# Linear attention: the order of output product and query product, and who takes the third output tile

## The chip, the cores and the metric

One Trainium2 chip, one core of it. The metric is the device time of one launch in microseconds (us).

## The reference, cut to what matters

The whole program is a two-layer "macaron" transformer on x of shape (4, 1024, 256): a quantised feed-forward (added at half weight), linear attention, the quantised feed-forward again, then a routed MLP, softmax attention and the routed MLP again. The change is inside the linear attention of the first layer:

```
q, k, v = x @ Wq.T + bq, x @ Wk.T + bk, x @ Wv.T + bv      # 16 heads of 128, 4 of them for k and v
sq, sk = elu(q) + 1, elu(k) + 1                            # "phi"
kv = einsum('bhsd,bhse->bhde', sk, v)
attn = einsum('bhsd,bhde->bhse', sq, kv) / (einsum('bhsd,bhd->bhs', sq, sk.sum(s)) + 1e-6)
x = x + attn.reshape(b, s, 16 * 128) @ Wo.T
```

## The kernel before, in words

Every fp32 product is made as three products of rounded halves (`split3`, lines 35 to 37), so each operand has a "hi" and a "lo" tile. The phase of this case is `linear_attention_phase`. It runs 128 steps, t = 0 to 127 (batch x head x half of the 1024 tokens, 512 tokens a step), with some 20 steps ahead of it and 4 behind it. The output projection is folded into the key-value matrix first (tile `li_m`), so a step of one half head adds straight to x. What one step does:

- TensorE (block at line 1281): the QUERY product of step t (6 matmuls of 512 columns into one PSUM bank), then the OUT product of step m = t - 2 (LAG = 2; 4 token tiles, 3 matmuls of 258 columns each, one bank a tile), then the jobs of the step (KV in 56 of the 128 steps, SUM, TURN, MADE, N, and background jobs of the neighbouring layers QA, QB, FA, X).
- ScalarE (line 1151): rounds phi of the step before to `li_phi_hi` (L1154), evicts jobs, then relu and exp on the query bank (L1162, L1165), copies the norm column of the four OUT banks (L1171), the KV activations (L1176 to L1184), background work, and last scales the fourth OUT tile into `li_ybuf` (L1191), for which it waits on VectorE's reciprocal.
- VectorE (line 1255): evicts jobs, KV work (L1262), layernorm of the neighbours (`normalise`), background, then finishes phi (`li_f`, L1267), takes the reciprocal of the norm (L1275), and scales and adds three OUT tiles into x (L1279).
- GpSimd (line 1094), a step later: `li_phi_lo` (L1098), adds the fourth tile to x (L1104), `li_kv_lo` (L1108), the split of query weights in the first 32 steps (L1084, L1087), MLP weight splits (L348, L350), and background: the bias add on eight x tiles at once (L378) among it.

The eight PSUM banks are one ring, given out in the order in which `step_claims` (line 893) and `linear_rows` name the claims. A claim waits until the bank of eight claims earlier is empty (`wait_emptied`), and the counter it waits for belongs to the engine that reads that bank last: `phi` is VectorE's L1267, `x` is L1279, `y3` is ScalarE's L1191. With five claims a step, the third OUT tile of a step takes the bank of the QUERY of the step before. Buffers: `li_f` 2, `li_phi` 3, `li_ybuf` 2, `li_rnorm` 1. SyncE loads weights in step order; its list is not moved.

Of the kernel before, what the change touches and what calls it, by code (L numbers as in the profile page):

```python
# [892 lines left out]
def step_claims(t):  # L893


    if 0 <= t < LOOP * B:
        yield ("QUERY", t), "phi", t + 1
    m = t - LAG
    if 0 <= m < LOOP * B:
        for j in range(3):  # L900
            yield ("OUT", m, j), "x", 3 * m + j + 1
        yield ("OUT", m, 3), "y3", m + 1


def linear_attention_phase(nc, sh, c, kv, a):
# [17 lines left out]
    with ExitStack() as ctx:  # L923
        def sb(name, shape, dt):
            return ctx.enter_context(nc.sbuf_tensor(f"li_{name}", shape, dt))
# [24 lines left out]
        bias_in = sb("bias_in", [P, H], F32)  # L950
        bias = sb("bias", [P, 2, H], F32)
        norm = sb("norm", [P, TC], F32)
        rnorm = sb("rnorm", [P, TC], F32)
        ybuf = sb("ybuf", [P, 2, D], F32)
        raw = sb("raw", [P, 2, D], F32)
        ps = ctx.enter_context(nc.psum_tensor("li_ps", [P, 8, CH], F32))

        c.begin(sh, "lc", plan, [ps[:, i, :] for i in range(8)], lambda b: TB * b)
# [34 lines left out]
        def ready(dve, kind, b):  # L993


            if kind == "QA":
                dve.wait_ge(sh.x_in[b], 16)
            if kind == "QB":
                dve.wait_ge(s_x, 3 * LOOP)
                dve.wait_ge(s_x3, LOOP)  # L1000

        c.ready = ready

# [7 lines left out]
        def _(sp):  # L1011
# [41 lines left out]
            for t in range(BEGIN, plan.end):  # L1053
                if t % 2 == 0 and 0 <= t < 2 * H:
                    keep_wq(t // 2)
                if t - 1 in made_time:
                    i = made_time[t - 1]
                    if i < 2 * KVH:
                        keep_wo(i)
                    if i + 1 < 2 * KVH:  # L1060
                        load_wo(i + 1)
                    elif i + 1 < 2 * KVH * B:
                        fetch_wo(i + 1)
                if t % 2 == 0 and 0 <= t and t // 2 + 2 < H:
                    load_wq(t // 2 + 2)
                if t % 2 == 0 and H <= t // 2 + 1 < B * H:
                    fetch_wq(t // 2 + 1)
                for part, v in mlp_pieces(c, t):
                    if n >= 2:
                        sp.wait_ge(s_split, n - 1)  # L1070
                    sp.dma_start(raw[:, n % 2, :], mlp_source(a, part, v)).then_inc(s_raw[n % 2], 16)
                    n += 1

        @block.gpsimd
        def _(pool):
# [18 lines left out]
            for t in range(BEGIN, plan.end):  # L1094
# [4 lines left out]
                                            ALU.subtract).then_inc(s_pl, 1)  # L1099
                if y_step(t - 1):  # L1100
                    m = t - 1 - LAG
                    pool.wait_ge(s_y3, m + 1)
                    x = x_tile_of(m, 3)
                    nc.gpsimd.tensor_tensor(x, ybuf[:, m % 2, :], x, ALU.add).then_inc(s_x3, 1)  # L1104
                if t - 3 in kv_time:
                    k, v, i = kv_time[t - 3]
                    pool.wait_ge(s_kvh, k + 1)
# [18 lines left out]
        def _(act):  # L1126
# [24 lines left out]
            for t in range(BEGIN, plan.end):  # L1151
# [2 lines left out]
                    nc.scalar.activation(ph[:, (t - 1) % (LAG + 1), :], f[:, (t - 1) % 2, :], ACT.Copy).then_inc(s_ph, 1)  # L1154
                evict(t)
                act_evict(nc, act, c, t)
                if q_step(t):
                    act.wait_ge(s_q, t + 1)
                    act.wait_ge(s_bias, 2)
                    if t >= 2:  # L1160
                        act.wait_ge(s_pl, t - 1)
                    nc.scalar.activation(f[:, t % 2, :], c.own_bank(("QUERY", t)), ACT.Relu, scale=-1.0,  # L1162
                                         bias=bias[:, 0, t // 2 % H:t // 2 % H + 1]).then_inc(s_uq, 1)
                    act.wait_ge(s_uq, t + 1)
                    nc.scalar.activation(f[:, t % 2, :], f[:, t % 2, :], ACT.Exp, scale=-1.0).then_inc(s_eq, 1)  # L1165
                if y_step(t):
                    act.wait_ge(s_y, t - LAG + 1)
                    if t > LAG:
                        act.wait_ge(s_rn, t - LAG)
                    for own, banks in out_banks(t - LAG):  # L1170
                        last = nc.scalar.activation(norm[:, own], ps[:, banks, D], ACT.Copy, bias=ATT_EPS)  # L1171
                    last.then_inc(s_norm, 1)
                if t - 1 in kv_time:
                    k, v, i = kv_time[t - 1]
                    act.wait_ge(c.taken, by_dve["KV", v, i])
# [7 lines left out]
                        old_sums(act, v)  # L1183
                    nc.scalar.activation(kvh[:, i, 0:2 * PK], z[:, k % 3, :], ACT.Copy).then_inc(s_kvh, 1)  # L1184
                act_background(nc, act, c, t)
                if y_step(t):
                    m = t - LAG
                    act.wait_ge(s_rn, m + 1)
                    if m >= 2:
                        act.wait_ge(s_x3, m - 1)  # L1190
                    nc.scalar.activation(ybuf[:, m % 2, :], c.own_bank(("OUT", m, 3))[:, 0:D], ACT.Copy, scale=rnorm[:, 3:4]).then_inc(s_y3, 1)  # L1191
                if made_time.get(t + 1, 2 * KVH) < 2 * KVH:
                    i = made_time[t + 1]
                    act.wait_ge(s_wo, 16 * i + 16)
# [6 lines left out]
        def _(dve):  # L1201
# [53 lines left out]
            for t in range(BEGIN, plan.end):  # L1255
                evict(t)
                dve_evict(nc, dve, sh, c, t)
                if t - 2 in kv_time:
                    k = kv_time[t - 2][0]
                    dve.wait_ge(s_ek, 2 * k + 2)  # L1260
                    zk = z[:, k % 3, 0:PK]
                    nc.vector.scalar_tensor_tensor(zk, zk, 1.0, ekk[:, k % 2, :], ALU.add, ALU.max).then_inc(s_phik, 1)  # L1262
                normalise(t)
                dve_background(nc, dve, sh, c, t)
                if q_step(t):
                    dve.wait_ge(s_eq, t + 1)
                    nc.vector.scalar_tensor_tensor(f[:, t % 2, :], c.own_bank(("QUERY", t)), bias[:, 1, t // 2 % H:t // 2 % H + 1], f[:, t % 2, :],  # L1267
                                                   ALU.add, ALU.max).then_inc(s_f, 1)
                if y_step(t):
                    m = t - LAG  # L1270
                    dve.wait_ge(s_norm, m + 1)
                    if m:
                        dve.wait_ge(s_y3, m)
                        dve.wait_ge(s_x, 3 * m)
                    nc.vector.reciprocal(rnorm[:], norm[:]).then_inc(s_rn, 1)  # L1275
                    dve.wait_ge(s_rn, m + 1)
                    for j in range(3):
                        x = x_tile_of(m, j)
                        nc.vector.scalar_tensor_tensor(x, c.own_bank(("OUT", m, j))[:, 0:D], rnorm[:, j:j + 1], x, ALU.mult, ALU.add).then_inc(s_x, 1)  # L1279

        @block.tensor
        def _(pe):
# [34 lines left out]

            pe.wait_ge(s_ones, 2 * TB)
            for t in range(BEGIN, plan.end):
                if q_step(t):  # L1320
                    if t % 2 == 0 and t // 2 < H:
                        pe.wait_ge(s_wql, t // 2 + 1)
# [6 lines left out]
                        last = split3(nc, c.own_bank(("QUERY", t)), wqh[:, t // 2 % 2, ws], wql[:, t // 2 % 2, ws],  # L1329
                                      xh[:, t // LOOP % 2, k, ts], xl[:, t // LOOP % 2, k, ts], start=(k == 0), stop=(k == KT - 1))  # L1330
                    last.then_inc(s_q, 1)
                if y_step(t):
                    m = t - LAG
                    head = m // 2 % H
                    pe.wait_ge(s_pl, m + 1)
                    if m % 4 == 0:
                        pe.wait_ge(c.taken, by_dve["MADE", m // LOOP * KVH + head // GQ, head // 2 % 2])
                    for j in range(TC):
                        wait_emptied(pe, c, plan.claim["OUT", m, j])
                        ts = slice(j * P, (j + 1) * P)  # L1340
                        last = split3(nc, c.own_bank(("OUT", m, j))[:, 0:MW], ph[:, m % (LAG + 1), ts], pl[:, m % (LAG + 1), ts],
                                      mh[:, head, :], ml[:, head, :], start=True, stop=True)
                    last.then_inc(s_y, 1)
                for kind, v, part in rows.get(t, []):
                    job(kind, v, part)
                pe_background(nc, pe, sh, c, t)
# [513 lines left out]
```

## Time and profile before

| | us |
|---|---|
| median of 3 runs | 3533.94 (3533.3 to 3534.62) |
| the profiled execution's own time | 3533.81 |
| its span | 3532.1 |
| the 128 steps, from the first relu (96.85) to the last | some 618 |

The span starts with the program's first instruction. In the views a line has a start or a count, then engine, source line, operation and tiles, where `out<-in` are names in the program with `li_` for this phase; matmul entries overlap, so the start-to-start distance of two matmuls is what one costs.

### The profile page before, as it was taken

What the parts mean: (1) busy time and instruction counts of PE and PEld (TensorE: products, weight loads), DVE (VectorE), ACT (ScalarE), POOL (GpSimd) and SP (SyncE); (2) the same over time, 40 slices, a digit from 0 to 9 for tenths busy, and PEclk for the clock granted to TensorE, in tenths of its full rate; (3) what the DMA queues carried; (4) which work ended last, traced back from release to release, by engine and by line L of the source; (5) the groups of instructions that cost most, each with busy time, mean ns of one, the idle gap of its engine ahead of it and who ended that gap; (6) DMA issues with size and microseconds to landing.
All of it is one profiled execution on the core that took longest, in us unless ns stands there. A gap on an engine that the chain in (4) does not pass through costs nothing.

```text
span 3532.1 us, 52701 instructions
## 1 busy us (share of the span) xinstructions
PE 3343.3 (95%) x19398; PEld 2864.0 (81%) x19398; DVE 2663.9 (75%) x4951; ACT 2045.8 (58%) x3907; POOL 1054.9 (30%) x1268
## 2 busy tenths in 40 slices
PE   3898999989999999999999999999999999999993
PEld 3777878868888888888888888888888888888882
DVE  5788796767876787876778677886788767876764
ACT  3676767646556565556555656556555565556551
POOL 4786656631122122122121212212111221122103
PEclk8999999999999999999999999999999999999995
DMA  2221112110000000000000110000000000000001
GB/s 82 71 83 57 58 57 70 54 37 13 13 22 28 13 16 13 14 25 25 13 13 13 31 42 16 14 14 28 22 14 13 23 26 26 13 25 23 26 7 30
DMA packets 98525, 104.21 MB, mean 30 GB/s; under 512 B 10336, under 2 KB 88800, under 8 KB 98144
## 3 DMA queue, kind: packets, MB, share of 16 engines
q1 hardware_dynamic: 98272, 100.85, 9.6%
q8 instruction: 157, 2.57, 0.3%
q14 instruction: 96, 0.79, 0.1%
HBM read 87.18 MB, written 13.63 MB: 29 GB/s over the span
## 4 chain that ended last, share of the span: by engine, by line
PE 70%; DVE 5%; ACT 3%; issue 1%; POOL 0%; DMA 0%; DVEq 0%; SPq 0%; POOLq 0%; ACTq 0%
PE at_ps_job L1752 12%; PE at_ps_job L35 7%; PE at_ps_job L37 7%; PE at_ps_job L36 7%; PE at_ps_o L35 6%; PE at_ps_o L37 6%; PE at_ps_o L36 6%; PE at_ps_s L35 6%; PE at_ps_s L36 6%; PE at_ps_s L37 6%; DVE at_neg_max L1684 1%; ACT x_resident L1618 1%; DVE at_probT_lo L1629 1%; PE at_ps_job L645 1%; DVE at_oT_lo L1660 0%
## 5 line engine op out<-in xcount | busy, mean ns | idle before, releaser
L1575 ACT ACTIVATE at_probT_hi<-at_ps_job 128x512 fp32r<-128x512 f32 x1024 | 611.4, 598 | 890.2 <-PE at_ps_job L1752 887.8
L1629 DVE TENSOR_TENSOR at_probT_lo<-at_ps_job,at_probT_hi 128x512 fp32r<-128x512 f32 x1024 | 702.7, 686 | 275.6 <-ACT at_probT_hi L1575 265.1
L1618 ACT ACTIVATE x_resident<-at_ps_s,at_neg_max 128x1024 f32<-128x1024 f32 x512 | 570.7, 1115 | 151.1 <-DVE at_neg_max L1684 145.9
L1684 DVE TENSOR_REDUCE at_neg_max<-at_ps_s 128x1 f32<-128x1024 f32 x512 | 622.1, 1215 | 5.3
L1752 PE MATMUL at_ps_job<-ident,x_resident 128*128 128x128 f32 x4096 | 613.8, 272 | 5.0 <-DVE at_probT_lo L1629 3.2
L1752 PEld LDWEIGHTS at_ps_job<-ident,x_resident 128*128 128x128 f32 x4096 | 495.9, 140 | 97.7 <-issue 7.3
L35 PE MATMUL at_ps_o<-at_probT_hi,at_v_lo 128*128 128x512 f32 x1024 | 446.3, 436 | 8.9 <-DVE at_oT_lo L1660 7.8
L1558 POOL TENSOR_TENSOR at_w_hi<-at_w_raw,ch_cols 128x256 fp32r<-128x256 f32 x192 | 117.6, 613 | 1120.5 <-PE at_ps_job L37 1099.8
L35 PE MATMUL at_ps_s<-at_k_hi,at_q_lo 128*128 128x512 f32 x1024 | 445.1, 435 | 0.0
L37 PE MATMUL at_ps_o<-at_probT_lo,at_v_hi 128*128 128x512 f32 x1024 | 404.7, 395 | 0.0
L36 PE MATMUL at_ps_s<-at_k_hi,at_q_hi 128*128 128x512 f32 x1024 | 402.0, 393 | 0.0
L36 PE MATMUL at_ps_o<-at_probT_hi,at_v_hi 128*128 128x512 f32 x1024 | 402.0, 393 | 0.0
L37 PE MATMUL at_ps_s<-at_k_lo,at_q_hi 128*128 128x512 f32 x1024 | 401.9, 392 | 0.0
L1642 DVE SCALAR_TENSOR_TENSOR x_resident<-at_ps_job,at_row_inv,x_resident 128x256 f32<-128x256 f32 x512 | 223.5, 478 | 25.7 <-PE at_ps_job L37 11.9
L37 PEld LDWEIGHTS at_ps_s<-at_k_lo,at_q_hi 128*128 128x128 f32 x1024 | 192.2, 188 | 43.8
L37 PEld LDWEIGHTS at_ps_o<-at_probT_lo,at_v_hi 128*128 128x128 f32 x1024 | 192.2, 188 | 42.8
L35 PEld LDWEIGHTS at_ps_o<-at_probT_hi,at_v_lo 128*128 128x128 f32 x1024 | 193.4, 189 | 39.3 <-issue 17.6
L1098 POOL TENSOR_TENSOR li_phi_lo<-li_f,li_phi_hi 128x512 fp32r<-128x512 f32 x128 | 166.7, 1302 | 174.2 <-ACT li_phi_hi L1154 172.9
L35 PE MATMUL at_ps_job<-ch_xnT_hi,at_w_lo 128*128 128x512 f32 x512 | 203.5, 397 | 11.1 <-POOL at_w_lo L1560 10.0
L36 PEld LDWEIGHTS at_ps_s<-at_k_hi,at_q_hi 128*128 128x128 f32 x1024 | 194.4, 190 | 22.8
L35 PEld LDWEIGHTS at_ps_s<-at_k_hi,at_q_lo 128*128 128x128 f32 x1024 | 193.4, 189 | 22.9
L36 PEld LDWEIGHTS at_ps_o<-at_probT_hi,at_v_hi 128*128 128x128 f32 x1024 | 194.5, 190 | 19.9
(274 smaller groups left out, 7485.9 us busy)
## 6 DMA issues: line engine op xcount, KB each, us to landing
at_w_raw<-attn_w SPq DMA_DIRECT2D x256, 128.0 KB, 2.3
at_w_raw<-mlp_w SPq DMA_DIRECT2D x112, 128.0 KB, 2.3
li_wo_hi<-li_wo_kept SPq DMA_DIRECT2D x24, 256.0 KB, 2.7
li_wo_lo<-li_wo_kept SPq DMA_DIRECT2D x24, 256.0 KB, 3.0
li_wq_hi<-li_wq_kept SPq DMA_DIRECT2D x48, 128.0 KB, 2.2
li_wq_lo<-li_wq_kept SPq DMA_DIRECT2D x48, 128.0 KB, 2.8
x_resident<-x SPq DMA_DIRECT2D x4, 1024.0 KB, 13.1
out<-x_resident SPq DMA_DIRECT2D x4, 1024.0 KB, 4.9
```

Of the source, the lines that this page charges most:

```text
L35: nc.tensor.matmul(out, al, bh, start=start, stop=False)
L36: nc.tensor.matmul(out, ah, bh, start=False, stop=False)
L37: return nc.tensor.matmul(out, ah, bl, start=False, stop=stop)
L645: nc.tensor.matmul(out[:, k * P:(k + 1) * P], c.tiles[:, j, k * P:(k + 1) * P], c.hot[:, j, :], start=(j == 0), stop=(j == TB - 1))
L1098: nc.gpsimd.tensor_tensor(pl[:, k % (LAG + 1), :], f[:, k % 2, :], ph[:, k % (LAG + 1), :].bitcast(F32), ALU.subtract).then_inc(s_pl, 1)
L1558: nc.gpsimd.tensor_tensor(hi, src, none, ALU.add).then_inc(s_wh[part], 1)
L1575: nc.scalar.activation(ph[:, i // TC, 4 * half:4 * half + 4, (i % TC) * P:(i % TC + 1) * P], c.turned_bank(2 * TB * u + 2 * i + half), ACT ...
L1618: nc.scalar.activation(prob[:, slot % 2, :], ps_s[slot % 2][:], ACT.Exp, bias=nmax[:, slot:slot + 1], accum_out=rsum[:, u % 2, slot:slot + ...
L1629: nc.vector.tensor_tensor(pl[at], c.turned_bank(2 * TB * u + 2 * i + half), ph[at].bitcast(F32), ALU.subtract).then_inc(s_pl, 1)
L1642: last = nc.vector.scalar_tensor_tensor(x, src[:, j * D:(j + 1) * D], rinv[:, v % 2, tile:tile + 1], x, ALU.mult, ALU.add)
L1684: nc.vector.tensor_reduce(nmax[:, slot:slot + 1], ps_s[slot % 2][:], AX.X, ALU.max, negate=True).then_inc(s_max, 1)
L1752: last = nc.tensor.transpose(turned[:, j, :], prob[:, i % 2, kt * P:(kt + 1) * P], sh.ident[:])
```

## The change

OUT is claimed and issued ahead of QUERY on TensorE. ScalarE copies the norm ahead of relu and exp, and scales two tiles (the third and the fourth) right behind exp, ahead of the KV activations. VectorE does the reciprocal and two x tiles at the start of its step, and phi last. GpSimd adds two tiles a step. `rnorm` and `ybuf` are doubled; the room for it comes from letting the MLP weight load share `wq_raw`.

The diff's core, in the order GpSimd, ScalarE, VectorE behind the buffers. Left out are the places that the moved blocks leave (on ScalarE the norm copy behind exp and the scaling at the step's end, on VectorE the reciprocal and three tiles behind phi), TensorE's OUT block, which moves unchanged ahead of its `if q_step(t)`, two waits in `ready` that follow the new counts, and a wait of the first MLP loads for the end of the query weight splits.

```diff
 def step_claims(t):
+    m = t - LAG
+    if 0 <= m < LOOP * B:
+        for j in range(2):
+            yield ("OUT", m, j), "x", 2 * m + j + 1
+        for j in range(2, 4):
+            yield ("OUT", m, j), "y3", 2 * m + j - 1
     if 0 <= t < LOOP * B:
         yield ("QUERY", t), "phi", t + 1
-    m = t - LAG
-    if 0 <= m < LOOP * B:
-        for j in range(3):
-            yield ("OUT", m, j), "x", 3 * m + j + 1
-        yield ("OUT", m, 3), "y3", m + 1
...
-        rnorm = sb("rnorm", [P, TC], F32)
-        ybuf = sb("ybuf", [P, 2, D], F32)
-        raw = sb("raw", [P, 2, D], F32)
+        rnorm = sb("rnorm", [P, 2, TC], F32)
+        ybuf = sb("ybuf", [P, 2, 2, D], F32)
+        raw = wq_raw
...
                 if y_step(t - 1):
                     m = t - 1 - LAG
-                    pool.wait_ge(s_y3, m + 1)
-                    x = x_tile_of(m, 3)
-                    nc.gpsimd.tensor_tensor(x, ybuf[:, m % 2, :], x, ALU.add).then_inc(s_x3, 1)
+                    for j in range(2):
+                        pool.wait_ge(s_y3, 2 * m + j + 1)
+                        x = x_tile_of(m, 2 + j)
+                        nc.gpsimd.tensor_tensor(x, ybuf[:, m % 2, j, :], x, ALU.add).then_inc(s_x3, 1)
...
                 act_evict(nc, act, c, t)
+                if y_step(t):
+                    act.wait_ge(s_y, t - LAG + 1)
+                    if t > LAG:
+                        act.wait_ge(s_rn, t - LAG)
+                    for own, banks in out_banks(t - LAG):
+                        last = nc.scalar.activation(norm[:, own], ps[:, banks, D], ACT.Copy, bias=ATT_EPS)
+                    last.then_inc(s_norm, 1)
                 if q_step(t):
...
                 if y_step(t):
...
+                    m = t - LAG
+                    act.wait_ge(s_rn, m + 1)
+                    if m >= 2:
+                        act.wait_ge(s_x3, 2 * m - 2)
+                    for j in range(2):
+                        nc.scalar.activation(ybuf[:, m % 2, j, :], c.own_bank(("OUT", m, 2 + j))[:, 0:D], ACT.Copy,
+                                             scale=rnorm[:, m % 2, 2 + j:3 + j]).then_inc(s_y3, 1)
...
             for t in range(BEGIN, plan.end):
                 evict(t)
                 dve_evict(nc, dve, sh, c, t)
+                if y_step(t):
+                    m = t - LAG
+                    dve.wait_ge(s_norm, m + 1)
+                    if m >= 2:
+                        dve.wait_ge(s_y3, 2 * m - 2)
+                        dve.wait_ge(s_x, 2 * m - 2)
+                    nc.vector.reciprocal(rnorm[:, m % 2, :], norm[:]).then_inc(s_rn, 1)
+                    dve.wait_ge(s_rn, m + 1)
+                    for j in range(2):
+                        x = x_tile_of(m, j)
+                        nc.vector.scalar_tensor_tensor(x, c.own_bank(("OUT", m, j))[:, 0:D], rnorm[:, m % 2, j:j + 1],
+                                                       x, ALU.mult, ALU.add).then_inc(s_x, 1)
```

## Rows read from the trace of the kernel before

**Rows 1.** The page, section 1: busy us (share of the span) xinstructions

```profile
PE 3343.3 (95%) x19398; PEld 2864.0 (81%) x19398; DVE 2663.9 (75%) x4951; ACT 2045.8 (58%) x3907; POOL 1054.9 (30%) x1268
```

**Rows 2.** Busy time in stretches of eight steps; its first line names the columns

```profile
core 0: us, PE busy (x) PEld busy (x) DVE busy (x) ACT busy (x) POOL busy (x), PEclk, DMA share, GB/s
...
416.15:457.27 41.12, 39.17 (x208) 32.23 (x207) 39.78 (x89) 31.32 (x73) 28.20 (x26) 1.00 0.24 75
...
495.83:536.28 40.45, 38.36 (x206) 32.02 (x204) 39.39 (x91) 28.86 (x70) 22.05 (x21) 1.00 0.23 72
...
657.18:685.12 27.94, 27.74 (x173) 24.49 (x171) 25.29 (x66) 20.12 (x48) 17.49 (x18) 1.00 0.29 91
685.12:711.69 26.57, 24.97 (x145) 20.60 (x143) 23.24 (x48) 17.97 (x44) 14.16 (x14) 1.00 0.08 21
sum 614.84, PE 571.85 PEld 490.66 DVE 501.03 ACT 436.78 POOL 422.42; mean PE 35.74 PEld 30.67 DVE 31.31 ACT 27.30 POOL 26.40
```

**Rows 3.** Waits, 100 to 716 us: who for whom, total us, times, longest us

```profile
ACT li_ybuf L1191 <- DVE li_rnorm L1275: 120.2, 91, 6.4
...
PE li_ps L35 <- DVE li_f L1267: 32.1, 29, 4.5
...
PE li_ps L35 <- POOL li_phi_lo L1098: 5.2, 6, 1.2
```

**Rows 4.** Timeline of TensorE, step 61: start us, us taken, line, tiles

```profile
403.43 0.40 PE L35 MATMUL li_ps<-ch_xnT_hi,li_wq_lo 128*128 128x512 f32 x1
...
404.60 0.40 PE L37 MATMUL li_ps<-ch_xnT_lo,li_wq_hi 128*128 128x512 f32 x1
404.84 0.28 PE L35 MATMUL li_ps<-li_m_hi,li_phi_lo 128*128 128x258 f32 x1
...
406.28 0.27 PE L1307 MATMUL li_ps<-ident,li_kvs 128*128 128x128 f32 x1
```

**Rows 5.** Timeline of ScalarE in the same step: the first relu after that

```profile
405.04 0.69 ACT L1162 ACTIVATE li_f<-li_ps,li_bias 128x512 f32<-128x512 f32 x1 [1.06 <-PE li_ps L37]
```

**Rows 6.** Timeline of all engines, steps 126 and 127

```profile
708.55 0.68 ACT L1162 ACTIVATE li_f<-li_ps,li_bias 128x512 f32<-128x512 f32 x1
...
709.26 0.63 ACT L1165 ACTIVATE li_f<-li_f 128x512 f32<-128x512 f32 x1
...
709.93 0.75 DVE L1267 SCALAR_TENSOR_TENSOR li_f<-li_ps,li_bias,li_f 128x512 f32<-128x512 f32 x1 [1.00 <-ACT li_f L1165]
...
710.59 0.17 DVE L1275 RECIPROCAL li_rnorm<-li_norm 128x4 f32<-128x4 f32 x1
...
711.17 0.62 ACT L1154 ACTIVATE li_phi_hi<-li_f 128x512 fp32r<-128x512 f32 x1
...
711.69 0.68 ACT L1162 ACTIVATE li_f<-li_ps,li_bias 128x512 f32<-128x512 f32 x1
711.86 1.26 POOL L1098 TENSOR_TENSOR li_phi_lo<-li_f,li_phi_hi 128x512 fp32r<-128x512 f32 x1 [1.15 <-ACT li_phi_hi L1154]
```

**Rows 7.** Groups of GpSimd in the phase: xcount, busy us, mean ns, idle before

```profile
L1098 POOL TENSOR_TENSOR li_phi_lo<-li_f,li_phi_hi 128x512 fp32r<-128x512 f32 x128 | 166.7, 1302 | 174.2 <-ACT li_phi_hi L1154 172.9 <-POOL ch_r_rounded L350 0.9
L1104 POOL TENSOR_TENSOR x_resident<-li_ybuf,x_resident 128x256 f32<-128x256 f32 x127 | 99.4, 783 | 0.0
...
L378 POOL TENSOR_TENSOR x_resident<-x_resident,quant_bias_half 128x2048 f32<-128x2048 f32 x3 | 13.9, 4645 | 0.0
...
L350 POOL TENSOR_TENSOR ch_r_rounded<-li_raw,ch_r_rounded 128x256 fp32r<-128x256 f32 x16 | 11.7, 734 | 1.3
```

**Rows 8.** Groups of VectorE in the phase, same columns

```profile
L1279 DVE SCALAR_TENSOR_TENSOR x_resident<-li_ps,li_rnorm,x_resident 128x256 f32<-128x256 f32 x381 | 161.0, 478 | 4.5
...
L1211 DVE TENSOR_TENSOR li_z<-li_ps,li_bkv 128x512 f32<-128x512 f32 x56 | 38.1, 680 | 1.6 <-POOL li_kv_lo L1108 1.6
```

**Rows 9.** Source line 97: duration ns min/median/max, first and last start

```profile
L97 DVE TENSOR_SCALAR ch_r<-x_resident,ln_mean,ln_rstd x40: 400/824/1381, 116.7 to 698.8; 128x256 f32<-128x256 f32 x40
L97 DVE TENSOR_SCALAR li_xn<-x_resident,ln_mean,ln_rstd x24: 400/698/4640, 153.3 to 497.1; 128x256 f32<-128x256 f32 x24
```

More of the change, by code:

```diff
@@ L998, in ready @@
             if kind == "QB":
-                dve.wait_ge(s_x, 3 * LOOP)
-                dve.wait_ge(s_x3, LOOP)
+                dve.wait_ge(s_x, 2 * LOOP)
+                dve.wait_ge(s_x3, 2 * LOOP)
         c.ready = ready
@@ L1070, in _ @@
                         sp.wait_ge(s_split, n - 1)
+                    else:
+                        sp.wait_ge(s_wql, H)
                     sp.dma_start(raw[:, n % 2, :], mlp_source(a, part, v)).then_inc(s_raw[n % 2], 16)
@@ L1166, in _ @@
                 if y_step(t):
[L1167 to L1172, printed above, removed]
+                    m = t - LAG
[5 more added lines that the diff above has]
+                                             scale=rnorm[:, m % 2, 2 + j:3 + j]).then_inc(s_y3, 1)
                 if t - 1 in kv_time:
@@ L1185, in _ @@
                 act_background(nc, act, c, t)
[L1186 to L1191, printed above, removed]
                 if made_time.get(t + 1, 2 * KVH) < 2 * KVH:
@@ L1268, in _ @@
                                                    ALU.add, ALU.max).then_inc(s_f, 1)
[L1269 to L1279, printed above, removed]
         @block.tensor
@@ L1319, in _ @@
             for t in range(BEGIN, plan.end):
+                if y_step(t):
+                    m = t - LAG
+                    head = m // 2 % H
+                    pe.wait_ge(s_pl, m + 1)
+                    if m % 4 == 0:
+                        pe.wait_ge(c.taken, by_dve["MADE", m // LOOP * KVH + head // GQ, head // 2 % 2])
+                    for j in range(TC):
+                        wait_emptied(pe, c, plan.claim["OUT", m, j])
+                        ts = slice(j * P, (j + 1) * P)
+                        last = split3(nc, c.own_bank(("OUT", m, j))[:, 0:MW], ph[:, m % (LAG + 1), ts], pl[:, m % (LAG + 1), ts],
+                                      mh[:, head, :], ml[:, head, :], start=True, stop=True)
+                    last.then_inc(s_y, 1)
                 if q_step(t):
@@ L1331, in _ @@
                     last.then_inc(s_q, 1)
[L1332 to L1343, printed above, removed]
                 for kind, v, part in rows.get(t, []):
```

## The prediction

> **What bounds the kernel now.** I read the page first, then the busy time by stretch, the waits, and the timelines of single steps. TensorE is busy for 95% of the span [rows 1]; the change touches the 128 steps of linear attention alone, so I look for TensorE's idle time there. In the 127 measured steps TensorE is busy 571.85 of 614.84 us, VectorE 501.03, ScalarE 436.78, GpSimd 422.42 [rows 2]: 4.84 us a step, 43 us of it without a matmul. The waits say what ended them: 32.1 us on phi, VectorE's `li_f` (29 times), 5.2 us on GpSimd's `li_phi_lo` (6 times) [rows 3]. The first is the bank ring: an OUT tile takes the bank of the QUERY before. What is late behind it is VectorE, which is busy 39.78 of 41.12 us and 39.39 of 40.45 us in steps 64 to 71 and 80 to 87 [rows 2]. ScalarE's 120.2 us of waiting for the reciprocal [rows 3] is long and harmless: ScalarE has time.
>
> All sums are made against the profiled execution, 3533.81 us; it stands 0.13 us under the median of the runs, so nothing is corrected. A difference of 0.2% (7 us) is about what a measurement of this kernel can tell from none.
>
> **1. OUT ahead of QUERY: the time allowed to phi.** The query product takes 404.84 - 403.43 = 1.41 us of TensorE, the OUT product 406.28 - 404.84 = 1.44 us [rows 4]. Between the end of QUERY t and OUT t there stood two OUTs and two QUERYs, 5.70 us, and the jobs of two steps; now there stand OUT t-1 and QUERY t+1, 2.85 us, and the same jobs. The chain that must fit: the last query matmul ends at 404.60 + 0.40 = 405.00, relu starts 0.04 later [rows 4, 5]; relu to exp 0.71; exp to `li_f` 0.67; `li_f` takes 0.75 and `li_phi_hi` follows in 0.04 where nothing stands before it (it did: 711.17 - 709.93 = 1.24, with the scaled tile between); `li_phi_hi` to `li_phi_lo` 0.69; `li_phi_lo` 1.26 and some 0.05 to TensorE [rows 6]. Sum 4.21 us. Two steps then take at least 1.44 + 1.41 + 0.16 + 4.21 = 7.22 us, 3.61 a step, where jobs are few. The last 15 steps take 27.94/8 = 3.49 and 26.57/7 = 3.80 now [rows 2]. The first eight of them lose 8 x 0.12 = **1 us**. Bounds: 0, if the chain is never last; 8 us, if all some 50 steps with few jobs lose that and 0.05 at each restart.
>
> **2. Two adds on GpSimd in a queue that phi uses.** An add is 0.783 us [rows 7]; 127 more are 99 us, and 422 + 99 = 521 of 615 us busy: no bound on average, but `li_phi_lo` stands in that queue behind everything. The longest is the bias add of 4.65 us, three times. At such a step the queue is 1.30 (`li_phi_lo`) + 1.57 (two adds) + 4.65 + 1.30 [rows 7] = 8.8 us, and 0.79 + 0.69 go before it: 10.3 us from the start of one `li_f` to the end of the next `li_phi_lo`. Three steps of 4.84 less the 4.43 from a step's start to its `li_f` (1.44 + 1.41 + 0.16 + 0.04 + 0.71 + 0.67) leave 10.1 us after the change, and less if `li_f` is late. Before, with QUERY first, it was 14.52 + 1.41 - 2.99 = 12.9. So each costs a few tenths to 1.5 us, 3 us together. The MLP weights are split by 16 pairs of operations, the second of each 0.73 us [rows 7], two pairs in a step; such a step asks 2.9 + 2.8 us of GpSimd and more with KV, against 4.84: another 3 us, and 1 us for the query weight splits of the first steps. Term: **+7 us**. Bounds: 0; 22 us, if eight clusters lose 2 us and the three long adds 2 each.
>
> **3. A tile less on VectorE, and a round trip more.** One of three tiles goes: 161.0/381 = 0.42 us [rows 8]. But the reciprocal stood behind `li_f` at once (710.59 - 709.93 = 0.66 us from start to start) and now waits for a norm copy that ScalarE makes behind `li_phi_hi`, which waits for `li_f`: 0.79 + 0.52 (711.69 - 711.17) + 0.17 + 0.04 = 1.52 us [rows 6]. That is 0.86 us of hole in each step that VectorE sets. In a KV step the bank eviction of 38.1/56 = 0.68 us [rows 8] fits into it, so 0.18 - 0.42 = -0.24; in another step it is 0.86 - 0.42 = +0.44. Where ScalarE also evicts a MADE or N bank ahead of the norm copy the hole widens by half a us, every other KV step, and eats what the KV steps won. With some 12 steps without KV set by VectorE: **+5 us**. Bounds: -13 us (the 0.42 in full in 32 saturated steps, rival A) and +10.
>
> **4. Two-sided use of SBUF by VectorE and GpSimd.** Layernorm's line 97 takes 0.40 us at best, 0.82 or 0.70 in the median and once 4.64 us [rows 9], as long as GpSimd's bias add of 4.65 [rows 7]: it waits while GpSimd works. Its 64 instances take about (40 x 0.82 + 24 x 0.70 + 3.9) / 64 = 0.84 us, 0.44 over the best; with GpSimd busy 521 instead of 422 us the excess grows by a quarter, 64 x 0.10 = 6 us of VectorE, a third of it where VectorE is last: **+2 us**. Bounds 0 and 6. The Trainium skill, "SBUF — State Buffer", section "Who interferes with whom", has it as an exclusive lock: a VectorE operation with two SBUF inputs or in a 2-port mode and a GpSimd operation exclude each other, so moving work from the one to the other gives part of it back. The trace agrees for line 97, by the 4.64 us.
>
> **5. The ring's wait.** An OUT tile now takes the bank of a QUERY two steps old, so the wait for `li_f` goes. Late next is `li_phi_lo`: it comes 0.79 + 0.69 + 1.26 + 0.05 = 2.8 us after the start of `li_f`, one step later. In a KV step of 4.3 us that is the same moment for TensorE as the old wait; in a lighter one it is later. What really goes is the wait in KV steps for OUT banks, which L1279 frees only behind phi. Steps 64 to 71 and 80 to 87 have 1.95 + 2.09 us of idle TensorE [rows 2]; the 56 KV steps then have 14, and I take half: **-7 us**. Bounds: 0 and -20 (two thirds of the 32.1 us of rows 3).
>
> **6. The rest.** ScalarE gets a second tile: cover is its idle time, 615 - 437 us [rows 2]; 127 tiles of half a us leave 115 idle. Where it is full for a few steps (gelu, quantised tiles) I count **+2 us**, bounds 0 and 5. The shared load buffer waits for splits that end 60 steps earlier, the two doubled buffers and the new counts hide nothing: 0, covered by that distance. SyncE's list doesn't move.
>
> **Sum:** 1 + 7 + 5 + 2 - 7 + 2 = +10 us, **3544 us**.
>
> **Rival A, faster (30%).** VectorE is the one late engine, and the tile off it and the ring's freedom arrive: -13 (part 3) and -7 to -20 (part 5), against +3 to +10 of parts 1 and 2: 3517 us. For it: 32.1 us of waits name `li_f`, 5.2 name GpSimd. Against it: the hole of part 3, which is on the same engine. It decides if ScalarE's norm copy reaches VectorE while it still evicts. The Trainium skill, "Perfetto Trace Analysis", section "Optimizing Scalar/DVE Operations", states the rule for it: with VectorE saturated, moving work to ScalarE may pay; it adds that a move to GpSimd may not.
>
> **Rival B, they cancel (26%).** Parts 2 and 3 cost half of what I count: within 7 us of 3534.
>
> **Rival C, phi on GpSimd becomes the bound (10%, a part of slower).** Parts 1 and 2 near their upper bounds, 8 + 22, others as forecast: 3566 us. For it: the allowance halves while the queue grows by a third. Against it: GpSimd now waits 172.9 us for `li_phi_hi` [rows 7].
>
> **How the numbers follow.** The forecast, slower by 3 to 20 us, has 34%; it and C make slower 44%, with same 26% and faster 30%. The forecast's own range is 3537 to 3554. The range for 8 in 10 reaches from 3515 (rival A, a tenth left below) to 3567 (C, a tenth above).
>
> **What would show it.** Right: TensorE's wait for `li_f` near 0, its waits for `li_phi_lo` at 15 us or more; VectorE's reciprocal with idle time before it, released by the norm copy, 0.2 to 0.9 us a step; steps 112 to 119 at 3.6 us or above; line 97's mean higher. Wrong: waits for `li_phi_lo` under 10 us in total, or steps 64 to 87 shorter by over 0.25 us each, which is rival A.

## The result, and the profile after

| | us |
|---|---|
| changed kernel, median of 4 runs | 3589.16 (3586.68 to 3590.16) |
| kernel before, median of 4 runs on the same chip | 3533.62 (3532.89 to 3534.62) |
| ratio | 1.0156, 95% interval 1.0138 to 1.0174 |
| the profiled execution's own time, its span | 3586.68, 3585.0 |

The change makes the kernel 55.5 us slower. The forecast was 3544, slower by 10, with a range up to 3567: the side was right, the size was not. Of all the executions behind this document one, of the kernel with LAG 3 and the evictions first below, took 9029.98 us; its other three lie between 3554.06 and 3554.12, and its profile is not read.

Section 1 of the page, to read against [rows 1]:

```profile
PE 3351.6 (93%) x19398; PEld 2863.0 (80%) x19398; DVE 2609.7 (73%) x4823; ACT 2093.9 (58%) x4033; POOL 1142.4 (32%) x1396
```

128 instructions left VectorE, 126 came to ScalarE, 128 to GpSimd, and TensorE has the same number. TensorE was busy 3343.3 us and is busy 3351.6, so most of the loss is idle time. Busy time by stretch, from first relu to first relu, for the steps of [rows 2] (its first line names the columns; the last is all 127 steps):

```profile
core 0: us, PE busy (x) PEld busy (x) DVE busy (x) ACT busy (x) POOL busy (x), PEclk, DMA share, GB/s
...
444.64:487.64 43.00, 39.21 (x209) 31.16 (x207) 36.14 (x77) 34.44 (x82) 32.90 (x33) 1.00 0.20 62
702.43:736.20 33.77, 29.88 (x167) 25.04 (x166) 23.17 (x62) 23.50 (x54) 24.35 (x28) 0.95 0.20 63
736.20:763.59 27.39, 23.26 (x142) 19.14 (x140) 17.86 (x39) 20.99 (x49) 17.04 (x19) 1.00 0.08 20
95.88:763.59 667.71, 580.42 (x3335) 489.55 (x3334) 448.31 (x997) 483.96 (x1132) 507.65 (x536) 0.96 0.19 58
```

The 127 steps take 667.7 instead of 614.8 us [rows 2]: all of the 52.9 us by which the span grew lie here. TensorE's idle time grew from 42.99 to 87.29 us, by 44.3. The other 8.6 us are in its busy time, for equally many matmuls, at a mean granted clock of 0.96 where it was 0.97. Four stretches of 2 us around one hole of the changed kernel show a way to that (columns as above):

```profile
256.00:258.00 2.00, 0.00 (x0) 0.00 (x0) 1.97 (x2) 1.57 (x4) 2.00 (x1) 1.00 0.33 83
258.00:260.00 2.00, 0.22 (x1) 0.22 (x2) 1.35 (x3) 0.58 (x2) 2.00 (x3) 1.00 0.16 52
260.00:262.00 2.00, 2.00 (x13) 2.00 (x13) 0.29 (x1) 0.22 (x2) 2.00 (x3) 0.63 0.00 0
262.00:264.00 2.00, 2.00 (x6) 1.60 (x6) 1.05 (x3) 0.23 (x2) 1.72 (x3) 0.52 0.00 0
```

From 256 to 260 us TensorE was busy for 0.22 us; from 260 to 264 it was busy all the time at a granted clock of 0.63, then 0.52, near the lower of its two levels (1.2 GHz). How much of the 8.6 us is the clock, no run separates. VectorE is no longer full: it is busy 36.14 of 43.00 us in steps 64 to 71, where it was 39.78 of 41.12 [rows 2]. The work of the three smaller engines is spread better, and the steps are longer. So I looked at the waits, here from 96 to 764 us (who for whom, total us, times, longest):

```profile
PEld li_ps L35 <- POOL li_phi_lo L1101: 84.6, 61, 5.5
...
DVE li_rnorm L1270 <- ACT li_norm L1166: 67.7, 57, 4.3
...
PE li_ps L35 <- POOL li_phi_lo L1101: 62.6, 51, 5.1
DVE li_m_lo L1233 <- ACT li_m_hi L1149: 49.1, 31, 3.1
...
DVE ch_r L479 <- POOL x_resident L384: 15.4, 7, 3.2
DVE li_m_lo L1226 <- ACT li_m_hi L1143: 15.2, 14, 1.7
...
ACT li_ybuf L1183 <- DVE li_rnorm L1270: 7.3, 7, 2.5
PE li_ps L35 <- DVE li_f L1285: 6.0, 5, 4.0
```

TensorE's wait for `li_f` fell from 32.1 to 6.0 us, and its wait for `li_phi_lo` rose from 5.2 to 62.6 [rows 3]. One wait of VectorE is new, 67.7 us for ScalarE's norm copy, and one has grown to 49.1 us, for `li_m_hi`: ScalarE takes the high half of that bank, and VectorE's low half needs it. In the kernel before the second was

```profile
DVE li_m_lo L1227 <- ACT li_m_hi L1145: 13.9, 31, 1.6
```

One step from the timeline of the changed kernel without TensorE (start, us taken, engine, line, tiles, in brackets the idle time ahead of it and its releaser):

```profile
448.89 0.69 ACT L1173 ACTIVATE li_f<-li_ps,li_bias 128x512 f32<-128x512 f32 x1 [1.05 <-PE li_ps L37]
...
449.61 0.63 ACT L1176 ACTIVATE li_f<-li_f 128x512 f32<-128x512 f32 x1
...
450.14 0.82 ACT L1183 ACTIVATE li_ybuf<-li_ps,li_rnorm 128x256 f32<-128x256 f32 x2
450.27 0.75 DVE L1285 SCALAR_TENSOR_TENSOR li_f<-li_ps,li_bias,li_f 128x512 f32<-128x512 f32 x1
...
450.86 0.41 ACT L1188 ACTIVATE li_ekk<-li_z 128x256 f32<-128x256 f32 x1
...
451.30 0.42 ACT L1190 ACTIVATE li_ekk<-li_ekk 128x256 f32<-128x256 f32 x1
451.62 0.62 ACT L452 ACTIVATE ch_r<-ch_r 128x512 f32<-128x512 f32 x1
452.14 0.62 ACT L1158 ACTIVATE li_phi_hi<-li_f 128x512 fp32r<-128x512 f32 x1
452.32 1.29 POOL L389 TENSOR_TENSOR x_resident<-ch_r,x_resident 128x512 f32<-128x512 f32 x1 [1.55 <-ACT ch_r L452]
452.67 0.58 ACT L1149 ACTIVATE li_m_hi<-li_ps 128x512 fp32r<-128x512 f32 x1
453.14 0.22 ACT L1166 ACTIVATE li_norm<-li_ps 128x2 f32<-128x2 f32 x2
453.28 0.69 DVE L1233 TENSOR_TENSOR li_m_lo<-li_ps,li_m_hi 128x512 fp32r<-128x512 f32 x1 [2.26 <-ACT li_m_hi L1149]
453.57 1.31 POOL L1101 TENSOR_TENSOR li_phi_lo<-li_f,li_phi_hi 128x512 fp32r<-128x512 f32 x1
```

`li_f` starts at 450.27. In [rows 6] `li_phi_hi` followed after 1.24 us and `li_phi_lo` 0.69 later. Here `li_phi_hi` starts 1.87 us after `li_f`, behind work of ScalarE that is not part of phi, and `li_phi_lo` 1.43 later, behind a background add. From the start of relu to the end of `li_phi_lo` it is 454.88 - 448.89 = 5.99 us, where the prediction's chain has 4.21 - 0.04 - 0.05 = 4.12. VectorE stands still for 2.26 us of that, because the bank that it is to read is evicted behind `li_phi_hi`.

### The profile page after: what moved, and what is told of

The parts are those of the page before. It is cut to its first block, busy times and chain, and to the rows that moved or that the text cites. A ratio compares the mean times of both kernels' runs of the same rounds, so it can differ in the third digit from the quotient of the medians.

```text
span 3585.0 us, 52826 instructions
## 1 busy us (share of the span) xinstructions
PE 3351.6 (93%) x19398; PEld 2863.0 (80%) x19398; DVE 2609.7 (73%) x4823; ACT 2093.9 (58%) x4033; POOL 1142.4 (32%) x1396
## 4 chain that ended last, share of the span: by engine, by line
PE 69%; DVE 5%; ACT 3%; issue 1%; POOL 0%; DMA 0%; DVEq 0%; SPq 0%; POOLq 0%; ACTq 0%
PE at_ps_job L1759 11%; PE at_ps_job L35 7%; PE at_ps_job L37 7%; PE at_ps_job L36 6%; PE at_ps_o L35 6%; PE at_ps_o L37 6%; PE at_ps_o L36 6%; PE at_ps_s L35 6%; PE at_ps_s L36 6%; PE at_ps_s L37 6%; DVE at_neg_max L1691 1%; ACT x_resident L1625 1%; DVE at_probT_lo L1636 1%; PE at_ps_job L645 1%; DVE at_oT_lo L1667 0%
## 5 line engine op out<-in xcount | busy, mean ns | idle before, releaser
L35 PE MATMUL li_ps<-li_m_hi,li_phi_lo 128*128 128x258 f32 x512 | 161.5, 315 | 69.6 <-POOL li_phi_lo L1101 64.7
L35 PE MATMUL at_ps_job<-ch_xnT_hi,at_w_lo 128*128 128x512 f32 x512 | 203.5, 397 | 11.9 <-POOL at_w_lo L1567 10.9
```

The source lines that it names most:

```text
L35: nc.tensor.matmul(out, al, bh, start=start, stop=False)
```

## The experiments

"Order" is the change without the moved tile (three tiles on VectorE, one add on GpSimd); "tile" is the moved tile in the old order. All were timed beside the kernel before, whose median is 3533.1 to 3534.7 us in each set; where a difference is taken across sets, it can be off by about that spread. The expectations name theories by letters, and some kernels by number: e1 is the order alone, e2 the tile alone, e5 the tile with the short add, e6 the kernel before with the scaled tile behind `li_phi_hi`, e15 the changed kernel with LAG 3 and the evictions first.

### The two parts, and their return to the old place

Three kernels. The order alone (shown for VectorE; the claims, the counts, ScalarE's one tile and GpSimd's one add follow):

```diff
-                    for j in range(2):
+                    for j in range(3):
                         x = x_tile_of(m, j)
```

> The changed kernel with three tiles on VectorE and one on GpSimd, as before: the new order alone. Theory A (the order: phi's allowance at TensorE is too short) and theory C (the round trip from phi over ScalarE's norm copy back to VectorE): 3575 to 3590 us, nearly all of the 55 us. Theory B (GpSimd's second add stands ahead of phi_lo): 3545 us or less, and TensorE's wait for li_phi_lo under 25 us instead of 64.7.

The tile alone: the ring, TensorE and VectorE as before, with

```diff
-                    nc.scalar.activation(ybuf[:, m % 2, :], c.own_bank(("OUT", m, 3))[:, 0:D], ACT.Copy, scale=rnorm[:, 3:4])...
+                    for j in range(2):
+                        nc.scalar.activation(ybuf[:, m % 2, j, :], c.own_bank(("OUT", m, 2 + j))[:, 0:D], ACT.Copy, scale=rnorm[:, 2 + j:3 + j])...
```

> The kernel before with its own order, and only the third tile moved to ScalarE and GpSimd. Theory B: 3560 us or more. Theories A and C: within 8 us of 3534, or faster (rival A of the prediction: down to 3520), since VectorE has 0.42 us less a step and phi its old allowance.

And the changed kernel with QUERY ahead of OUT again on TensorE and in the claims:

```diff
+                if q_step(t): ...
                 if y_step(t): ...
-                if q_step(t): ...
```

> The changed kernel, but TensorE issues and claims QUERY ahead of OUT again; ScalarE, VectorE and GpSimd keep the new order. Theory A: 3540 to 3560 us, most of the loss back, and TensorE's wait for li_phi_lo under 20 us. Theory C: 3580 us or more, since the round trip stays (and VectorE's first work of a step now waits for an OUT that comes 1.4 us later).

Measured: order 3580.8 us (ratio 1.0119 to 1.015), **+47**; tile 3569.65 (1.0087 to 1.0117), **+36**; QUERY first 3602.26 (1.0178 to 1.0209), +69. So theory A missed its 3540 to 3560, and theory C's "3580 us or more" holds; in that kernel TensorE waits 91.4 us for `li_f`. For the tile theory B holds, A and C missed. Each part alone costs more than the 10 us that were forecast for both, and together they cost 28 less than their sum. TensorE's order as such is not the whole cause: with the other engines as they are after the change, QUERY first is slower still.

### TensorE's order alone

The kernel before with nothing changed but OUT ahead of QUERY on TensorE and in `step_claims`.

```diff
 def step_claims(t):
-    if 0 <= t < LOOP * B:
-        yield ("QUERY", t), "phi", t + 1
...
         yield ("OUT", m, 3), "y3", m + 1
+    if 0 <= t < LOOP * B:
+        yield ("QUERY", t), "phi", t + 1
```

> The kernel before, with OUT claimed and issued ahead of QUERY on TensorE and nothing else changed. Theory A: 3560 us or more, and waits of TensorE for li_phi_lo of 40 us or more. Theory E (what costs in e1 is that VectorE does phi last and waits for the norm first; TensorE's order fits either way): within 12 us of 3534.

Measured: 3662.08 us (1.0344 to 1.0378), **+129**. Its waits from 96 to 830 us:

```profile
ACT li_f L1162 <- PE li_ps L37: 236.4, 122, 3.8
...
PE li_ps L35 <- DVE x_resident L1279: 132.7, 105, 4.8
...
PEld li_ps L35 <- POOL li_phi_lo L1098: 9.8, 14, 2.1
```

With five claims a step, QUERY now takes the bank of the second OUT tile of the step before, and VectorE frees that one (L1279) only behind phi of that step. QUERY, relu, exp, `li_f`, reciprocal, tiles, next QUERY is one ring, and 132.7 us of TensorE's waits name it. TensorE hardly waits for `li_phi_lo`, so both expectations missed: the time is on theory A's side, for a reason that neither had. With this ring of banks OUT can go first cheaply only if VectorE's tiles go first as well, as the change has it.

### The allowance of phi

One more step between phi and the product that reads it. The three phi buffers stay three.

```diff
-LAG = 2
+LAG = 3
-        ... (LAG + 1) ...
+        ... 3 ...
```

On the changed kernel, on the order alone, and on the kernel before as a control:

> The changed kernel with OUT three steps behind QUERY instead of two (three buffers for phi still suffice). Theory A: phi has a whole step more, 3555 us or less, TensorE's waits for li_phi_lo under 10 us. Theories D and E (loops between VectorE and ScalarE that don't pass through OUT of the same step): 3575 us or more, with TensorE's waits moved to bank or query waits.

> The new order alone (three tiles on VectorE, one on GpSimd) with the output product a further step behind (LAG 3, three phi buffers as in both kernels). The order alone with LAG 2 took 3580.8, 47 over the kernel before. Theory P (phi's halved allowance is the larger part of the order's price): at or under 3557, TensorE's waits for li_phi_lo from 62.2 to under 5 us, waits for li_f not back. Theory S (the loop of ScalarE and VectorE, norm copy and eviction behind phi_hi, is the larger part): 3557 to 3575, with VectorE's waits for the norm copy and for li_m_hi still above 80 us together.

> Control: the kernel before with LAG 3. Its TensorE waits only 5.2 us for li_phi_lo, so a longer allowance has nothing to give if the 18.5 us that LAG 3 gave the changed kernel are the allowance's. If they are: 3530 to 3538. If LAG 3 helps in another way (other bank ring positions, slack for the reciprocal): under 3525, and then the 18.5 us are not the allowance's alone.

Measured: changed kernel 3570.69 us (1.0091 to 1.0121), **-18.5**; order 3562.9 (1.0066 to 1.01), **-17.9**; before 3532.79 (0.9987 to 1.0006), nothing. Waits of the changed kernel with LAG 3, 96 to 750 us:

```profile
DVE li_rnorm L1270 <- ACT li_norm L1166: 54.6, 54, 4.4
DVE li_m_lo L1233 <- ACT li_m_hi L1149: 48.6, 31, 3.1
PE li_ps L35 <- DVE li_f L1285: 18.6, 17, 4.0
...
PE li_ps L35 <- POOL li_phi_lo L1101: 2.0, 5, 0.7
```

The first lies between the expectations' 3555 and 3575, the second where theory S had it, the third as expected. 60 us of waits for `li_phi_lo` are gone and 18 us of time with them, while the wait for `li_f` rose from 6.0 to 18.6: two thirds of that wait was no price. The control shows that LAG 3 has no gain of its own. The order alone loses the same 18 with a single add in GpSimd's queue, so the allowance is the order's cost, not the add's. The rest of the order, 29 us, has another cause.

### The round trip between ScalarE and VectorE

Two ways to shorten it. VectorE makes the norm copy itself, straight from PSUM:

```diff
-                        last = nc.scalar.activation(norm[:, own], ps[:, banks, D], ACT.Copy, bias=ATT_EPS)
+                        last = nc.vector.tensor_scalar(norm[:, own], ps[:, banks, D], ATT_EPS, None, ALU.add)
```

> The changed kernel, but VectorE adds the epsilon to the norm itself, straight from PSUM, so it no longer waits for ScalarE's copy behind li_phi_hi. Theory C: 3560 us or less, VectorE's 70.8 us of waits for the norm copy gone. Theories A and B: 3580 to 3592 us (a small operation more on VectorE).

Or ScalarE evicts the banks of the jobs ahead of `li_phi_hi`, which waits for `li_f`:

```diff
+                evict(t)
+                act_evict(nc, act, c, t)
                 if q_step(t - 1):
                     act.wait_ge(s_f, t)
                     nc.scalar.activation(ph[...], f[...], ACT.Copy).then_inc(s_ph, 1)
-                evict(t)
-                act_evict(nc, act, c, t)
```

> The changed kernel, with ScalarE evicting jobs ahead of li_phi_hi. Theory F: VectorE's waits of 49.1 + 15.2 us for li_m_hi go and 20 us or more come back, 3569 us or less. Theory A' (the way from phi to OUT sets the step alone): 3585 us or more, since li_phi_hi comes no earlier.

Measured: VectorE's own norm 3591.72 us (1.0147 to 1.0181), no gain; evictions first 3577.23 (1.0105 to 1.0135), **-12**, between what the two theories expected. The first isn't a clean test. The wait of 67.7 us is gone, but VectorE waits 29.4 us for the OUT product instead, its wait for exp ahead of `li_f` rose from 29.8 to 46.6, and its own copy is 170 operations of 0.15 us, 26 us of new work. So it shows that this remedy gains nothing, not that the round trip costs nothing. The wait for `li_m_hi`, shorter, is worth something. I then took the allowance away as well, to see whether one hides the other:

> The changed kernel with both remedies: LAG 3 (3570.69 alone, -18.5) and ScalarE's job evictions ahead of phi_hi (3577.23 alone, -12). If phi's allowance and the loop of ScalarE and VectorE are two separate costs they add up: about 3559. If each hides behind the other: above 3565 (no more than the better of the two). If removing one lets the other give all of it: under 3550.

> As e15, and VectorE makes the norm copy itself (no gain alone, 3591.72). If the norm's round trip was hidden behind TensorE's wait for li_phi_lo, it is worth something now: 5 to 15 us under e15. If the round trip never set the step: within 3 of e15, or slower, as VectorE has an operation more.

> The order alone (three tiles on VectorE) with LAG 3 and ScalarE's evictions ahead of phi_hi. The order with LAG 3 took 3562.9, with VectorE waiting 42 us for li_m_hi and 51 us for the norm copy. If the evictions are a separate cost here too: 3545 to 3552. If the waits only move: over 3557.

Measured: 3554.11 us (1.0042 to 1.0075), 3553.57 (1.0042 to 1.0072), and 3541.64 for the order (1.0014 to 1.0032). LAG 3 and the evictions together give 35.1 us where 18.5 + 11.9 = 30.4 were to be had one by one: they are separate costs, and the second gives some 5 us more once the first is gone. The norm by VectorE gives nothing here either, with 178 operations of 0.15 us on VectorE (27 us). On the order the evictions give 3562.9 - 3541.64 = **21.3 us**, more than was expected, and leave it 8 us above the kernel before. That kernel isn't the fair measure for it, as the last group of experiments shows. Waits of this last kernel, 96 to 720 us:

```profile
DVE li_rnorm L1268 <- ACT li_norm L1164: 60.3, 76, 4.1
PE li_ps L35 <- DVE li_f L1283: 18.0, 14, 4.1
DVE li_m_lo L1231 <- ACT li_m_hi L1147: 11.5, 12, 1.7
...
PE li_ps L35 <- POOL li_phi_lo L1100: 2.6, 2, 1.6
```

### The add on GpSimd, apart from ScalarE's tile

GpSimd adds 8 of the 256 columns of the third tile; 248 are left out. Such an add takes 0.23 us instead of 0.77.

```diff
-                        nc.gpsimd.tensor_tensor(x, ybuf[:, m % 2, j, :], x, ALU.add)...
+                        cols = slice(0, D if j else 8)
+                        nc.gpsimd.tensor_tensor(x[:, cols], ybuf[:, m % 2, j, cols], x[:, cols], ALU.add)...
```

In the old order, in the changed kernel, and in the changed kernel with LAG 3 and the evictions first:

> e2 (tile moved, old order), but GpSimd adds only 8 of the third tile's 256 columns, some 0.2 us instead of 0.78; the other 248 are left out. Theory B (GpSimd's queue): 3545 us or less. Theory D (ScalarE's scaled tile stands in a serial loop: VectorE's phi, reciprocal, ScalarE's tiles, phi_hi, next relu and exp, next phi, so that each tile of 0.37 us comes on top): 3562 to 3570 us, nearly no change from e2's 3569.65.

> The changed kernel, with GpSimd adding only 8 of the third tile's 256 columns (the other 248 left out). Theory B (GpSimd's second add delays phi_lo): 3570 us or less, as the same cut gave 17 us back in the old order (e5 against e2). If GpSimd's queue is hidden in the new order: 3583 us or more.

> The changed kernel with LAG 3, ScalarE's evictions ahead of phi_hi, and the third tile's add cut to 8 of its 256 columns (248 are left out). e15 with the first two took 3554.11; the short add alone gave 23 on the changed kernel. Theory S (separate costs): 3531, and what is left against the best order of before (3513.96 with the same evictions) is ScalarE's second tile, 17 us. Theory P (the add costs through TensorE's wait for li_phi_lo, which LAG 3 has removed): over 3545.

Measured: 3552.23 us (1.0039 to 1.0069), **-17.4** against tile; 3565.91 (1.0075 to 1.0105), **-23.3** against the changed kernel; 3538.86 (1.0002 to 1.0021), **-15.3** against 3554.11. The first lies between the expectations of B and D, the second where B had it, the third between S and P. So 0.54 us less a step on GpSimd gives 15 to 23 us, and two thirds of that (15.3 of 23.3) even where TensorE no longer waits for `li_phi_lo`: that part of the add's cost is not phi's queue. What carries it isn't settled. VectorE's background behind GpSimd's adds is one candidate (L479 waits 15.4 us for L384 above, 8.9 before, 13.8 with the short add). Another is that VectorE's own operations get longer: in the 127 steps it is busy 448.31 us in the changed kernel and 434.37 with the short add, for the same work. Line 97 is 5.9 us of that, here in the changed kernel, 96 to 764 us (duration ns min/median/max):

```profile
L97 DVE TENSOR_SCALAR ch_r<-x_resident,ln_mean,ln_rstd x40: 400/734/1390, 117.6 to 749.9; 128x256 f32<-128x256 f32 x40
L97 DVE TENSOR_SCALAR li_xn<-x_resident,ln_mean,ln_rstd x24: 401/614/4717, 156.0 to 529.8; 128x256 f32<-128x256 f32 x24
```

and with the short add:

```profile
L97 DVE TENSOR_SCALAR ch_r<-x_resident,ln_mean,ln_rstd x40: 400/407/1386, 117.4 to 726.8; 128x256 f32<-128x256 f32 x40
L97 DVE TENSOR_SCALAR li_xn<-x_resident,ln_mean,ln_rstd x24: 401/408/4211, 154.8 to 516.3; 128x256 f32<-128x256 f32 x24
```

### ScalarE's place for its tiles, in the old order

Three kernels in the old order. The scaled tile goes behind `li_phi_hi` of the next step; then the same with the moved tile, both tiles there; then the first one with the evictions ahead of `li_phi_hi`.

```diff
                     nc.scalar.activation(ph[...], f[...], ACT.Copy).then_inc(s_ph, 1)
+                if y_step(t - 1):
+                    m = t - 1 - LAG
+                    act.wait_ge(s_rn, m + 1)
+                    ...
+                    nc.scalar.activation(ybuf[:, m % 2, :], c.own_bank(("OUT", m, 3))[:, 0:D], ACT.Copy, scale=rnorm[:, 3:4])...
```

> The kernel before, with one block moved on ScalarE: the fourth tile is scaled behind li_phi_hi of the same step instead of ahead of it, so phi_hi no longer waits for the reciprocal. Theory D: faster than before, 3500 to 3526 us, as a wait for VectorE's reciprocal (120.2 us in all) and 0.37 us leave the path from phi to phi_hi. If that path is not in a loop that sets the step: 3534 us within 6.

> e6 (the kernel before with the scaled tile behind li_phi_hi) with the third tile moved to ScalarE and GpSimd too. Theory D (the tile costs where ScalarE's tiles stand ahead of phi_hi): the move now costs GpSimd's part alone, 17 us or less on e6's 3518.72, that is 3536 us or less. If it costs for other reasons: 3550 us or more (e6 + 36).

> e6, with ScalarE evicting the jobs of the step before ahead of li_phi_hi. Theory F (VectorE stands idle for ScalarE's first half of an eviction, 12.4 + 11.2 us in e6, while ScalarE waits 99.6 us for VectorE's phi): 3505 to 3515 us. If the later phi_hi costs as much (0.5 us on its path where phi is not late): 3519 us or more.

Measured: 3518.72 us (0.9945 to 0.9975), **-14.4**: rows 3's wait of 120.2 us for the reciprocal, which I called harmless, stood ahead of `li_phi_hi`. With the moved tile there 3549.62 (1.0027 to 1.0061), 31 over that kernel where the tile cost 36 in its old place: a miss, the tile costs in this place too. With the evictions first **3513.96** (0.9928 to 0.9958), as expected, 4.8 less than without them, 19.6 us faster than the kernel before (3533.6) and 75 faster than the changed one: the best version of this study, and it has neither part of the change. It is also the fair measure for the new order. Both then have their scaled tile off the way to `li_phi_hi` and the evictions first, and the order has LAG 3 besides: 3541.64 - 3513.96 = 27.7 us remain, and no run divides them. In the 127 steps of the two TensorE is idle 49.3 against 32.8 us and busy 572.3 against 562.1, and VectorE's wait for the norm copy, 60.3 us in the new order, is 0.6 in this one. Its wait for `li_m_hi` (96 to 700 us) and TensorE's for `li_f`, 13.9 and 32.1 us before:

```profile
PE li_ps L35 <- DVE li_f L1267: 20.9, 18, 4.1
...
DVE li_m_lo L1227 <- ACT li_m_hi L1145: 1.9, 3, 0.7
```

## Why the prediction was wrong in size

The runs divide the 55.5 us. From the kernel before to the order +47.2; from there to the changed kernel with the short add 3565.91 - 3580.8 = -14.9; from that to the full add +23.3. Of the 47.2, LAG 3 takes back 17.9, which the control shows to be the allowance's, and the evictions ahead of `li_phi_hi` 21.3, of which the old order too had some 5 (4.8 in the one pair that was run). What is left isn't 8 but more: the new order also has its scaled tile out of the way of `li_phi_hi`, which alone gave the old one 14.4. Against the best old order 27.7 us stay open. The norm's round trip is the rival that no run excludes. Another order of the steps gives other sizes (the add is 15 to 23, the evictions 12 to 21), but the kinds stay.

1. **Part 1, OUT ahead of QUERY: the step that failed first.** The mechanism was right, the term was +1 with bounds 0 to 8, and it measured 18 (17.9 on the order, 18.5 on the changed kernel). The chain of 4.21 us was put together from steps 126 and 127 [rows 6], where the engines have no other jobs. In the step shown above the same stretch of it, 4.12 there, takes 5.99. The conclusion "eight of these steps lose 0.12 us each" rested on that best case; TensorE waited 51 times, 1.2 us each.
2. **Part 2, two adds on GpSimd.** Forecast +7 with an upper bound of 22; measured 15 to 23, for 0.54 of the add's 0.77 us. I counted only the few clusters where the queue is full. The loss doesn't need them, and most of it doesn't go through `li_phi_lo`, since it stays with LAG 3.
3. **Part 3, a tile less, a round trip more.** Right in kind, wrong in size. The gain of the tile does arrive in the new order: -14.9 for the whole move without most of its add, against my bound of -13. The norm's round trip, on which I put the loss, shows as 67.7 us of waits (0.53 a step, within the 0.2 to 0.9 forecast); what it costs isn't known, since the kernels that take it away put new work on VectorE (in the first, 26 us of operations for 21.5 us less of waiting: 67.7 + 29.8 became 29.4 + 46.6). The sentence on evictions ahead of the norm copy, "widens by half a us", stood nearest to a term that was shown: `li_m_lo` waits 49.1 us in 31 steps, 1.6 each, and its cure gives 12 to 21 us. The hole of 0.86 us came from the steps without jobs again; in the step shown above, with ScalarE's jobs between `li_f` and `li_phi_hi`, VectorE's hole ahead of `li_m_lo` is 2.26.
4. **Part 4, VectorE and GpSimd on SBUF.** For the change as a whole the sign was wrong. I forecast a longer line 97; its medians fell from 0.824 and 0.698 [rows 9] to 0.734 and 0.614 us, although GpSimd is busy 507.65 instead of 422.42 us. The mean, which I had put together as 0.84, was 49.87/64 = 0.78 and fell to 0.66. The order alone has 0.59 with GpSimd as busy as before (417.5 us), so the order shortens line 97 and the moved tile with its add lengthens it again, by 0.07, or 4.4 us of VectorE. In the old order the tile left it at 0.77. Which operations meet thus counts for at least as much as how busy GpSimd is. The Trainium skill, "SBUF — State Buffer", section "Who interferes with whom", with its exclusive lock, fits the longest instances, 4.64 and 4.72 us beside bias adds of 4.61 and 4.57; my scaling of the mean by GpSimd's busy share fits nothing.
5. **Part 5, the ring's wait.** It went as said, 32.1 to 6.0 us, and the wait for `li_phi_lo` is what is late next, also as said. I took -7 for it as time. With LAG 3 the wait for `li_f` is back at 18.6 us in a kernel that is 18.5 us faster: such a wait is where a late step shows, not a price. No run isolates the term, so whether any of it was earned stays open.
6. **Part 6, ScalarE's second tile under "its idle time".** In the old order this is false: the tile without the add costs 3552.23 - 3533.6 = +19, tile off VectorE included, and 0.23 us of the add still in it. I took the reason to be ScalarE's place between the reciprocal and `li_phi_hi`. But with both scaled tiles behind `li_phi_hi` the move costs 31 instead of 36 us, so the place explains little of it, and the rest stays open. In the new order, where it runs beside `li_f`, it is part of the -14.9. Idle time in total, 178 us, said nothing on either.

Of the rivals, A (faster) fell: steps 64 to 71 are 0.24 us longer each, not shorter. Its rule, that of the Trainium skill, "Perfetto Trace Analysis", section "Optimizing Scalar/DVE Operations", holds here for the one half (a tile from VectorE to ScalarE pays 15 us in the new order) and not in the old order. Its doubt about a move to GpSimd agrees with the 15 to 23 us of the add, though that the shared port is the reason isn't shown. C was nearest with 3566; it had phi on GpSimd as the bound, which is a third of the loss. Of the signs listed, four came (`li_f` near 0; `li_phi_lo` over 15; the reciprocal's idle time; steps 112 to 119 at 33.77/8 = 4.22 us) and one did not (line 97). They were written so wide that they would have come at +10 as well as at +55. The chances also overlap: a loss of 3 to 7 us belongs both to the forecast and to rival B.

The error common to parts 1, 3 and 6: durations from the emptiest steps, and one long wait [rows 3] read as slack. The 14.4 and 4.8 us that two moves on ScalarE gave the kernel before suggest that it was already held, in some steps, by a loop over two engines: `li_f`, `li_phi_hi`, evictions, VectorE's next step, `li_f`. No row of busy time shows that loop.

## What to carry to other kernels

Where two engines hand work back and forth in every step, cost a move by the chain through both, taken from a full step of the timeline and not from an empty one; a wait in an in-order queue is slack only if nothing behind it is waited for. Before moving work, look at what stands behind each wait: two moves in ScalarE's queue, evictions that are ready ahead of `li_phi_hi`, which waits, and the waiting scaled tile behind it, gave 20 us here, while the better spread of work cost 55. And bank claims in a ring have to be checked against the point at which the freeing engine gets to them: the order of two products alone cost 129 us.

## What the runs showed of the hardware

- A GpSimd add of 128x8 fp32 takes 0.23 us, one of 128x256 0.77 us.
- Line 97's 128x256 `tensor_scalar` on VectorE takes 0.40 us or up to 4.7 us: in the changed kernel the short add, 0.54 us less of GpSimd a step, takes the median of its group of 40 from 0.73 to 0.41 us, while `li_f` and the x tiles, which read PSUM, stay at 0.74 and 0.48 us in both kernels.
- In the changed kernel TensorE was busy for 0.22 us between 256 and 260 us; in the four us after that its granted clock was 0.63 and 0.52.
